# Turning gathered rows by on-chip copies and VectorE transposes, with copies and expert weights issued by one queue

## The reference

```python
y = x @ W_base.T + lora(x)              # a low-rank adapter chosen per sequence
probs = softmax(y @ gate_w.T)           # 16 experts
w, e  = top_k(probs, 2);  w = w / w.sum()
for the two chosen experts e of each token:
    h   = silu(y @ w_gate[e].T) * (y @ w_up[e].T)      # 512 -> 352
    out = out + w * (h @ w_down[e].T)                  # 352 -> 512
result = x + out
```

## Time and profile before

| | us |
|---|---|
| median of 3 runs | 362.03 (361.94 to 362.47) |
| the profiled execution, first to last instruction | 360.6 |
| PE busy | 348.6 (97%) |
| PEld busy | 309.4 (86%) |
| DVE busy | 198.2 (55%) |
| ACT busy | 179.5 (50%) |
| POOL busy | 135.5 (38%) |

### The profile page before, as it was taken

One profiled execution on the slowest core, in us unless ns is written; L12 is line 12 of the kernel. 1 busy time (PEld: TensorE's weight loads), 2 busy tenths in 40 slices (PEclk: granted clock), 3 DMA queues, 4 the chain that ended last, 5 costly groups with the idle time before them and its releaser, 6 DMA issues.

```text
span 360.6 us, 7506 instructions
## 1 busy us (share of the span) xinstructions
PE 348.6 (97%) x2007; PEld 309.4 (86%) x2007; DVE 198.2 (55%) x275; ACT 179.5 (50%) x242; POOL 135.5 (38%) x85
## 2 busy tenths in 40 slices
PE   8999999999999999999999999999999999999990
PEld 4777878789899999999999999999999998898970
DVE  0486799985638264544565536556282556556210
ACT  1588611524474554444764466464545457564320
POOL 0000000113634364655745437546264456532131
PEclk9999999999999999999999999999999999999996
DMA  8993865648497948678598684976929475920322
GB/s 296 391 450 118 320 239 186 234 143 307 149 362 225 276 87 262 155 219 229 121 291 263 188 257 77 297 211 184 334 42 307 106 222 159 304 42 7 55 34 37
DMA packets 28913, 73.78 MB, mean 205 GB/s; under 512 B 3440, under 2 KB 3568, under 8 KB 28784
## 3 DMA queue, kind: packets, MB, share of 16 engines
q1 hardware_dynamic: 19904, 54.30, 42.6%
q0 software_dynamic: 8960, 18.89, 23.8%
HBM read 60.59 MB, written 19.92 MB: 223 GB/s over the span
## 4 chain that ended last, share of the span: by engine, by line
PE 91%; DMA 3%; DVE 3%; issue 1%; POOLq 0%; ACT 0%; POOL 0%; DVEq 0%
PE bank L653 41%; PE bank L682 22%; PE bank L585 5%; PE bank L410 4%; PE bank L627 4%; PE bank L510 4%; PE bank L511 3%; PE bank L514 3%; DMA xg<-y_rows,gidx 2%; PE bank L426 1%; PE bank L441 1%; PE bank L537 1%; DMA y_rows<-y_st 1%; POOLq L92 0%; PE bank L571 0%
## 5 line engine op out<-in xcount | busy, mean ns | idle before, releaser
L1185 POOL DMA_INDIRECT out<-ys,sidx x40 | 81.2, 2030 | 123.4 <-ACT ys L813 57.3
L1164 POOL DMA_INDIRECT xg<-y_rows,gidx x40 | 53.8, 1345 | 95.5 <-issue 80.5
L348 DVE TENSOR_TENSOR w_lo<-w_raw,w_hi (+2 forms) x32 | 76.3, 2385 | 21.5 <-ACT w_hi L346 16.0
L653 PE MATMUL bank<-w_hi,xt_hi 128*128 x320 | 82.2, 333 | 0.2 <-issue 0.2
L653 PE MATMUL bank<-w_hi,xt_lo 128*128 x320 | 78.7, 322 | 0.0
L653 PE MATMUL bank<-w_lo,xt_hi 128*128 x320 | 78.6, 322 | 0.0
L346 ACT ACTIVATE w_hi<-w_raw (+2 forms) x32 | 64.8, 2024 | 9.4 <-issue 6.2
L653 PEld LDWEIGHTS bank<-w_hi,xt_lo 128*128 128x128 f32 x320 | 56.0, 188 | 0.0
L653 PEld LDWEIGHTS bank<-w_lo,xt_hi 128*128 128x128 f32 x320 | 56.0, 188 | 0.0
L804 ACT ACTIVATE sg<-bank 128x352 f32<-128x352 f32 x40 | 18.5, 463 | 74.5 <-PE bank L653 74.5
L653 PEld LDWEIGHTS bank<-w_hi,xt_hi 128*128 128x128 f32 x320 | 54.2, 189 | 0.8 <-issue 0.7
(11 more groups left out here) (178 smaller groups left out, 368.2 us busy)
## 6 DMA issues: line engine op xcount, KB each, us to landing
w_raw<-wall SPq DMA_DIRECT2D x16, 1408.0 KB, 7.5
w_raw<-wall SPq DMA_DIRECT2D x16, 768.0 KB, 10.6
x_st<-xt SPq DMA_DIRECT2D x8, 512.0 KB, 12.5
y_rows<-y_st SPq DMA_DIRECT2D x16, 256.0 KB, 4.0
head_sb<-head SPq DMA_DIRECT2D x2, 640.0 KB, 4.9
wb_sb<-wb SPq DMA_DIRECT2D x2, 512.0 KB, 8.4
wbt_sb<-wbt SPq DMA_DIRECT2D x2, 512.0 KB, 10.6
xg<-y_rows,gidx POOLq DMA_INDIRECT x40, 6.1
```

The source lines that it names most:

```text
L348: e.tensor_tensor(w_lo[:, bass.ds(dst, n)], raw, hi, ALU.subtract).then_inc(own, 1)
L653: mm = e.matmul(bank[2 + 2 * s + t % 2][:, 0:INTER], a, w[:, bass.ds(at + (k * GU + s * INTER), INTER)], start=k == 0 and i == 0, stop=k = ...
L1164: e.indirect_dma_start(out=xg[t % NXG][:], out_offset=None, in_=y_dram, in_offset=bass.IndirectOffsetOnAxis(ap=gidx[:, t:t + 1], axis=0)). ...
L1185: e.indirect_dma_start(out=out, out_offset=bass.IndirectOffsetOnAxis(ap=sidx[:, t:t + 1], axis=0), in_=ys[t % NYS][:], in_offset=None, bou ...
```

## The change

From tile 6 on (`N_PE = 6`), TensorE no longer turns x. A tile goes this way instead:

1. SyncE, once the gather of the tile has landed, issues four DMAs from `xg` into a new buffer `xs` (three of them): quarter q copies the columns q*128 to q*128+127 of all 128 rows into the 32 partitions q*32 to q*32+31, so each partition holds four tokens' 512-byte pieces.
2. VectorE turns `xs` in 32 x 32 blocks by one transpose instruction into `xt` (two buffers), at the end of iteration t for tile t+3 (`x_turned`). It reads and writes with a step of four values (16 bytes).
3. ScalarE (`x_evac`) and VectorE (`y_low`) split `xt` as they split `bank[0]` before, but for tile t+2 in iteration t and after `silu(t)` and `product(t)`.

Which hidden unit sits in which partition changes by this (unit 4i+k instead of 128k+i), so the weights are laid out accordingly on the host, and the TensorE transposes of tiles 0 to 5 read `xg` with a step of four values. The `dn` split of a tile moves on VectorE, from tile 6 on, from the end of the iteration before to its own iteration, behind `h_low`.

SyncE issues copies and weights in one order. For each t it issues the copies of tile t, then, if tile t-3 starts a run, the weights of the run after next, part by part: `gu` once the `gu` split of the run is done, `dn` once the `dn` split is done, and each only when the load of the same part before it has landed (one semaphore a part instead of two). A gather into `xg` waits for the copies of the tile eight before (from tile 6 on) instead of for TensorE.

```diff
+N_PE, NXS = 6, 3
+Q = 32
...
+        xs = [r_e(f"xs{i}", [P, H], F32) for i in range(NXS)]
+        xt = [r_e(f"xt{i}", [P, H], F32) for i in range(2)]
...
-        def load_weights(e, runs, r, parts=("gu", "dn")):
-
-            with e.If(runs > r) if r >= TOPK else nullcontext():
-                if r >= NRAW:
-                    e.wait_ge(v_dn, r - NRAW + 1)
-                ex = table(e, T_REX, r, 0, NEXP - 1)
-                for part in parts:
...
+        def x_rows(t):
+
+            return bank[0][:] if t < N_PE else xt[t % 2][:]
...
+            count = tile_count(e)
+
+            def later_weights(t):
+
+                run, new, at, _ = tile_word(e, t)
+                with e.If(new * SKIP + runs - run > SKIP + NRAW):
+                    ex = table(e, T_REX, bass.ds(run + NRAW, 1), 0, NEXP - 1)
+                    for part in PARTS:
+                        e.wait_ge(v_gu if part == "gu" else v_dn, run + 1)
+                        e.sem_inc(p_turn, 1)
+                        e.wait_ge(d_w[part], (run + NRAW) * 16)
+                        e.sem_inc(p_turn, 1)
+                        load_part(e, part, ex, at)
+
+            def rows_apart(t):
+
+                n = t - N_PE
+                with in_use(e, count, t):
+                    e.wait_ge(d_g[t % NXG], 16 * (t // NXG + 1))
+                    if n >= NXS:
+                        e.wait_ge(v_xr, n - NXS + 1)
+                    for q in range(P // Q):
+                        e.dma_start(xs[n % NXS][q * Q:(q + 1) * Q, :], xg[t % NXG][:, q * P:(q + 1) * P]
+                                    ).then_inc(d_xs[n % NXS], 16)
+
             e.wait_ge(d_g[N_LATE], 16)
-            for r in range(2, NEXP):
-                load_weights(e, runs, r)
-            count = tile_count(e)
+            for t in range(NTILE):
+                if t >= N_PE:
+                    rows_apart(t)
+                if 0 <= t - 3 < NTILE - NRAW:
+                    later_weights(t - 3)
...
-                        mm = e.transpose(bank[0][:, k * P:(k + 1) * P], xg[t % NXG][:, k * P:(k + 1) * P], ident)
+                        rows = xg[t % NXG][:].rearrange("p (r k) -> p k r", k=KH)[:, k]
+                        mm = e.transpose(bank[0][:, k * P:(k + 1) * P], rows, ident)
...
-                    if t + 1 < NTILE:
+                    if t + 1 < N_PE:
                         x_turn(e, count, t + 1)
...
+            def x_turned(t):
+                n = t - N_PE
+                with in_use(e, count, t):
+                    e.wait_ge(d_xs[n % NXS], (n // NXS + 1) * 16 * (P // Q))
+                    if n >= 2:
+                        e.wait_ge(v_xt, t - 1)
+                    e.transpose(xt[t % 2][:].rearrange("p (k i g) -> p g k i", k=KH, g=P // Q),
+                                xs[n % NXS][:].rearrange("p (g j k) -> p g k j", g=P // Q, k=KH)).then_inc(v_xr, 1)
...
```

More of the change, by code:

```diff
@@ L254, in build @@
         v_chain = sem("v_chain")
-        d_w = {part: [sem(f"d_{part}{i}") for i in range(NRAW)] for part in PARTS}
+        d_w = {part: sem(f"d_{part}") for part in PARTS}
+        d_xs = [sem(f"d_xs{i}") for i in range(NXS)]
+        v_xr = sem("v_xr")
         d_g = [sem(f"d_g{i}") for i in range(NXG)]
@@ L288, in table @@
         def table(eng, row, at, least, most):
-            return nc.values_load(tabs[0:1, row, at:at + 1], engines=[eng.engine], min_val=least, max_val=most,
+            cell = at if isinstance(at, bass.DynSlice) else slice(at, at + 1)
+            return nc.values_load(tabs[0:1, row, cell], engines=[eng.engine], min_val=least, max_val=most,
                                   skip_runtime_bounds_check_because="made on the chip, from counts that the shapes bound")
@@ L320, in split_weights @@
                 if act:
-                    e.wait_ge(d_w[part][0], 16)
+                    e.wait_ge(d_w[part], 16)
                     e.wait_ge(v_xlo, 2 * NBATCH)
@@ L328, in split_weights @@
             run, new, src, dst = word
[L329 to L338, removed]
-                    else:
-                        e.wait_ge(a_gu if gu else a_dn, run + 1)
-                    split_part(e, act, src + off, dst + off, n, own)
+            fresh = new > 0 if t < surely.get(e.engine, NFULL) else new * W_SLOT * 2 + count > W_SLOT * 2 + t
+            with e.If(fresh):
+                if act:
+                    e.wait_ge(d_w[part], (run + 1) * 16)
+                    if t < NSPLIT:
+                        e.wait_ge(m_tb, 2)
+                    else:
+                        e.wait_ge(m_gu if gu else m_dn, t - 2)
+                else:
+                    e.wait_ge(a_gu if gu else a_dn, run + 1)
+                split_part(e, act, src + off, dst + off, n, own)
         def split_part(e, act, src, dst, n, own):
@@ L358, in load_x @@
                 for i, half in enumerate(halves):
-                    load(x_st[b][:, half], xt[b][:, half], d_x[b][i])
+                    load(x_st[b][:, half], xin[b][:, half], d_x[b][i])
             load(head_sb[:], head, d_wt[0])
@@ L390, in _ @@
                     e.wait_ge(v_w12, 1)
-                    load_weights(e, runs, 1)
+                    for part in PARTS:
+                        e.wait_ge(d_w[part], 16)
+                        load_part(e, part, table(e, T_REX, 1, 0, NEXP - 1), 0)
                 if c == C_LOAD:
@@ L1248 @@
     x = get["x"]
[L1249 removed]
+    xin = x.reshape(NBATCH, SEQ, KH, P).transpose(0, 3, 2, 1)
     at = chunks(get["L0_cond_A"].reshape(RR, H).T)
@@ L1257 @@
     head, head2 = [np.concatenate([a.reshape(P, -1), w[:, :KH // 2].reshape(P, -1)], axis=1) for a, w in ((at, wt), (bw, wpt))]
-    gu = np.concatenate([get[n].transpose(0, 2, 1).reshape(NEXP, KH, P, INTER) for n in ("L0_ffn_w_gate", "L0_ffn_w_up")], axis=3)
+    gu = [get[n].transpose(0, 2, 1).reshape(NEXP, P, KH, INTER) for n in ("L0_ffn_w_gate", "L0_ffn_w_up")]
+    gu = np.concatenate([g.transpose(0, 2, 1, 3) for g in gu], axis=3)
     gu = gu.transpose(0, 2, 1, 3).reshape(NEXP, P, GUW)
```

58 lines of the change are left out of this document (36 added, 22 removed).

## The result

The changed kernel takes 371.12 us in the median of its runs (368.78 to 373.15), beside 361.99 (361.57 to 362.47) of the kernel before on the same chip: a ratio of 1.0248 [1.0213, 1.0282]. Forecast was 352.0 with a range of 346.5 to 359.0 and a chance of 0.09 for slower. The execution profiled took 372.97 us, 1.9 above that median, and has a span of 371.1 us, against 360.6 before and 351.0 in the sum of the prediction.

What follows compares the result with a forecast made beforehand. TensorE was taken to bound the kernel, at 91% of the chain. Sum: 360.6 − 14.8 − 0.3 + 0.3 + 0.5 + 4.7 = 351.0 us, plus 1.4 carried over: 352, range 346.5 to 359.0.

Steps and rivals of the forecast that it cites:

- The transposes off TensorE: TensorE, tiles 6 to 39: 34 times 0.436 us removed, 14.8 us gained, a tile then taking 6.21 us.
- SyncE's order in the steady part: SyncE's queue in steady runs: copies behind the dn weights land within VectorE's slack of 2 to 3 us; cost nothing.
- rival B: Steady part: copies behind dn land late at every run, 0.4 us for each of 13 runs, 5 us, 357; 13%.
- the second half: From the end of down(4) to the kernel's end; the forecast had 14.2 us gained there.
- The start: Around 110 to 123 us: TensorE waits 1.9 us through tile 6's copies, 2.8 through tile 7's; together 4.7 us lost.
- Weights leave later at the start: no cost: SyncE's weights at the start: every run has three tiles or more between load and split, so no cost.
- VectorE's transpose: VectorE, per tile: the added transpose of x takes 0.9 us, between 0.5 and 2.4.
- Rival C: VectorE becomes the bound, its transpose above 2.0 us; at 2.4 it costs 7 us, giving 359; 6%.
- The reads with a step on TensorE: TensorE's transposes of tiles 0 to 5, reading every fourth value: 0.3 us lost, between 0 and 2.6.
- The DMA load: DMA engines, per tile: copies at 35 ns a packet add 1.1 us, 5.9 of 6.2 busy; full but not the bound.
- rival D: DMA engines between tiles 8 and 36 become the bound, packets above 58 ns; at 70 ns about 376 us; 8%.

Runs made afterwards that it cites:

- e2: Changed kernel with every tile turned by TensorE, so no copies; the weights' new order and the reads with a step stay; 370.96 us, ratio 1.0268.
- x3: Kernel before in all but SyncE's order: weights part by part from the loop over tiles, dense reads, old weight layout; 367.22 us, ratio 1.0146.
- e1: Changed kernel with the copies of tile t+1 put ahead of the weights that stood behind those of tile t; 361.02 us, ratio 0.9966.
- x1: Changed kernel with only run 2's weights load put back ahead of the loop, behind the same gather as before the change; 367.85 us, ratio 1.0187.
- e3: Changed kernel with VectorE's transpose in dense blocks without a step, output not the reference's; 368.55 us, ratio 1.0223.
- e6: Changed kernel with only the dn part moved behind the next tile's copies, gu keeping its place; 364.76 us, ratio 1.0069.
- the fastest version: Changed kernel with dn behind the next tile's copies, run 2's load early and N_PE = 12; ten times 352.81 to 362.60 us, median 358.6.

## Why the prediction was wrong

**The transposes off TensorE (14.8 us): right in kind, a seventh too large.** 136 instructions are gone. But a free tile takes about 6.30 us, against 6.675 in the mean before (the prediction's 6.64 was the shorter of two in turn). So removing 0.436 brought 0.375, 2.0 us less over 33 tiles. `gate_up` no longer has its shorter turn of 3.81. Why is open; e2 shows 3.88 each time too, so it isn't the copies, and x3, with dense reads and the old layout of the weights, alternates again.

**SyncE's order in the steady part ("nothing"): this step failed.** Two things were wrong in it. The first is the landing. The prediction gave "6 to 8 us" for what is left of the weights and the copies behind them, against "some 8 us" until VectorE asks. From the issue of the `dn` part, the copies landed after 10.2 and 10.4 us in the two rounds shown, and after 10.2 to 11.4 in the seven rounds of the chain; 6 to 8 us fit only from the last of the copies' issues, 2.5 us after that of the `dn` part. That is the condition of rival B, held at 13%. The second is that the wait was held against VectorE's slack only once. It feeds itself: a late transpose makes the `dn` split behind it late, by that SyncE's `dn` weights, by that the copies behind them. So the slack isn't there anew for each run; the loop has a length of its own, 13.8 us for two tiles, and where it exceeds TensorE's 12.6 it sets the pace in the end. That is why B's price of 5 us was too low. The cost is what is left of the second half: 11.3 less 2.0, and less 0.7 us that the end behind the last `ys` took longer, 8.6 us. The trace has 8.8 of it between `down(6)` and `down(30)` (160.0 less 151.2), among them a wait for weights that SyncE issued late in the same way. Putting the copies ahead of the weights (e1) took 5.2 us off this stretch, and 10 off the whole kernel.

**The start (4.7 us): the right place, 8.8 us too small.** Right: tile 6's and then tile 7's copies, VectorE behind them, in that order. `down(4)` was to start at about 122.9 (118.31 and 4.6) and started at 129.62, 6.7 us later; the other 2.1 are TensorE's clock, which fell after the idle time and which no sum of dependences holds. The 6.7 come from the copies of tile 7, which landed at 126.2 where 119 was forecast. SyncE issued run 3's weights at 111.05 instead of 108.5, with branches and table reads between the copies of tile 6 and them; the last of tile 7's copies was issued at 115.8, and it took 10.3 us from there, where the forecast had counted the 10.6 us of the `dn` row from the weights' issue. "Weights leave later at the start: no cost" was wrong too, but it isn't part of these 8.8. Run 2's `gu` had nothing to spare, ScalarE waited 0.59 us for it before; it went out 1.1 us later and took 9.7 us instead of 7.1 (why is open). Where there are no copies this costs 4.6 us (x3). Here, behind it, VectorE waits for tile 6's copies anyway, and x1 shows `product(4)` only 0.85 us earlier without it.

**VectorE's transpose (0.9 us): 1.14, within the bounds, and no bound of the kernel.** Rival C needed 2.0. But 0.43 us of it is the step, and as part of the loop even that seems to cost some: 2.6 us by e3's median. By the Trainium skill's "SBUF — State Buffer", section on the DMA port swizzle, each access that crosses into a new 16-byte line costs; the runs agree that such a step costs, at 1.6 times for VectorE (1135 against 705 ns) and 1.5 for TensorE's weight loads (210 against 140).

**The reads with a step on TensorE (0.3 us for six tiles): about right.** 0.04 a tile in the group, about 0.1 with `gate_up`.

**The DMA load (5.9 of 6.2 us busy): rival D did not come.** The share was 0.85 here and 0.92 in e1, under the forecast 0.95, and a packet of the copies cost about 29 ns (queue 1 was busy 50.8% of 16 times 371.1 us where it was 42.6% of 16 times 360.6; the 558 us between, over 19584 packets), where 35 were taken and rival D's estimate was 46. The engines don't bound the mean. Single transfers do come late: SyncE waits 39 us for gathers in e1, some of which take over 8 us. That the high share makes them late is likely but not shown, since a gather took 8.23 us before as well.

## What to carry to other kernels

When a wait is added to an engine's program order, follow who waits behind it until the path either ends or comes back to the wait. If it comes back it is a loop, and its length against the iteration decides, not the slack on a single pass. In a queue that serves both a small urgent transfer and a large one that must wait for a semaphore, issue the small one first, and count the issuing engine's own time per round, for it can be the next bound (e6); and price a term as zero at the start of a pipeline only after reading the arrival and the use of what moves.

## What was not expected of the hardware

- TensorE ran `down(4)` in 4.20 us after 6.4 us without work where it takes 2.07, and x3's `gate_up` in 5.25 instead of 3.85 after 3.7: idle time cost a second time through the granted clock, which was 0.50 there, 2.1 and 1.4 us.
- Four 64 KB copies land 4.8 us after the start of the last issue with no weights right ahead of them (tile 6, 108.19 to 112.97), 7.1 to 8.9 behind a `dn` part, and 10.3 behind `gu` and `dn`.
- VectorE's transpose of 128 x 512 float32 in 32 x 32 blocks takes 705 ns dense and 1135 with a step of 16 bytes on both sides.
- The kernel's time lost its repeatability: 368.8 to 373.2 us after and 352.8 to 362.6 in the fastest version, against 361.4 to 362.5 before beside them. Crowded DMA engines don't explain it alone: x3, with no copies and a steady DMA share of 0.71, spreads from 364.5 to 369.2. It stays open.
